# VectorE's order at the opening of a turn in a macaron block: two low parts, attention's sum, the statistics and layer 4's result change places

## The chip, the cores and the metric

The kernel runs on 1 core of one Trainium2 chip. The metric is the device time of one execution in microseconds (us). TensorE does the matmuls, VectorE and ScalarE read its banks in PSUM, GpSimd works in SBUF alone, SyncE issues transfers. In the views below they are PE (PEld for its weight loads), DVE, ACT, POOL and SP; "DVEq" is VectorE's queue, that is its sequencer's own instructions.

## The reference, cut to what matters

x has 8 sequences of 512 tokens with 128 features. The block is a feed-forward net, a recurrent layer in attention's place, and the same feed-forward net again, each behind a layer norm and each added to x:

```python
def ffn(x):                                  # D 128, hidden 512
    h = silu(tlin(x, w1, s1)) * tlin(x, w2, s2)
    h = gelu(tlin(h, h1, sh1)); h = gelu(tlin(h, h2, sh2))
    return tlin(h, w3, s3)
x = x + 0.5 * ffn(layernorm(x))
x = x + attn(layernorm(x))     # h = tanh(x_t B + h A^T) over the tokens; y = h C; y W_out^T + b
x = x + 0.5 * ffn(layernorm(x))
```

## The kernel before, in words

The 4096 tokens are cut into 8 chunks of 512 columns. Each chunk passes the feed-forward net twice: 16 passes, g = 0 to 15, called turns here. Features or hidden units lie on the partitions, the chunk's tokens on the columns. Every layer's matmul takes its input as two float32r parts, the high part (y_hi, rounded by ScalarE or VectorE) and the low part (y_lo = y - y_hi, a TENSOR_TENSOR of VectorE, L705 and L700, or of GpSimd, L1271 and L1265). Layers 2 and 3 have 4 rows m of 4 steps k with 2 matmuls each (L256), layer 1 has 4 rows with two products (th's and u's bank), layer 4 has one row of 4 steps.

The order of the work is written out by hand on each engine; there is no scheduler. Turn g runs layers 2 and 3 of chunk g and layer 1 of chunk g + 1, and at its opening layer 4 of chunk g - 1. On TensorE the opening is: layer 2's row 0 with steps k = 0 and 1, attention's two matmuls (`attention`, L395), step k = 2, layer 4 of the chunk before (L256 in bank F1), the transposes of the next chunk's tokens (`front_tokens`, L274, from attention's sum lnin to bank FR), step k = 3. Then come the scan's matmul for step 0 (L388), row 1, scan step 1, row 2 (which overwrites layer 4's bank F1 and therefore waits for layer 4's result, `l4_out`), scan step 2, the transposes of the normalised features (`to_features`, L284, from xnt_f), row 3. Steps k of row 0 wait for y1's high and low part k: 0 to 2 from GpSimd, 3 from VectorE (`low1`, L700). Layer 4's step 3 waits for y3's low part 3 (`low`, L705). The token transposes wait for attention's sum (L732).

There are four kinds of turns. First-round turns 0 to 5 (`first_turn`, `early_turn`) have no attention; they transpose x1c, layer 4's result of the first pass, for the middle norm (L264). Three middle turns (`middle_turn`, c = 0, 1, 2) have both; with c = 1 and 2 the opening has attention's sum and the front statistics. Then follow turns of the second pass (`turn`, k = 1 to 7): 1 written out, 2 to 5 in a loop whose waits are against registers, 6 and 7 written out. Turn 7 has no next chunk and no attention. "Turn 1" to "turn 7" below are these; the middle turns are named as such.

The scan of the recurrent layer runs beside: a matmul per step (L388), two tanh of ScalarE (L1042, L1043) and a low part of VectorE (L724), which the next step's matmul waits for; a turn has 8 of them.

The front statistics (`front_stats`, L646) are four bn_stats (L630), a memset and four bn_aggr (L635) on VectorE; GpSimd makes 1/sqrt(var + eps) of them (ve L1257, rs L1260), VectorE normalises (L663) into xnt_f. Layer 4's result (`layer4`, L707, with its instruction at L719) is 0.5 s3 times the bank plus the residual, written to x1c or outb, and SyncE sends it off. In the end, when the scan's blocks agree, no further round is run; the profiled execution runs one. In turn 6 VectorE also compares the scan's ends (L974, L978) ahead of attention's sum.

VectorE's side of the end of a turn (before) and of the opening of a turn:

```python
772  gated(g + 1, KT - 1)          # y1's last part of the next chunk
773  y1_high(g + 1, KT - 1)
774  low1(g + 1)                   # its low part, L700
775  low(g, 3, y3_hi_r, ...)       # y3's last low part, L705
854  attention(att[0], att[1])     # the sum, L732
856  layer4(1, g - 1, k - 1)       # the result, L719
858  front_stats(g + 1)            # L630, L635
859  step(0); step(1)              # the scan's low parts, L724
862  normalise("f", g + 1, ...)    # L663
```

Of the kernel before, what the change touches and what calls it, by code (L numbers as in the profile page):

```python
# [35 lines left out]
CHUNKS = 8  # L36
# [20 lines left out]
def build(nc, xT, xtok, w1T, w2T, h1T, h2T, w3T, scales, Ablk, Brep, CTrep, WoutT, ident_d, mask_d, outT):  # L57
    with ExitStack() as ctx:
# [568 lines left out]
        def _(dve):  # L627
# [70 lines left out]
            def low1(g):  # L698
                dve.wait_ge(y1_hi_r[KT - 1], g + 1)
                nc.vector.tensor_tensor(y1_lo[:, KT - 1, :], y1[:, KT - 1, :], y1_hi[:, KT - 1, :].bitcast(F32),  # L700
                                        ALU.subtract).then_inc(y1_lo_dve, 1)
# [20 lines left out]
            def scan_low(n, t):  # L722
                dve.wait_ge(step_t, n * CSTEPS + t + 1)
                nc.vector.tensor_tensor(h[0:64, span(t)], SC[0:64, span(CSTEPS + t)], h[0:64, span(t)].bitcast(F32),  # L724
                                        ALU.subtract).then_inc(step_h, 1)
# [44 lines left out]
            def end_turn(g):  # L770

                gated(g + 1, KT - 1)
                y1_high(g + 1, KT - 1)
                low1(g + 1)
                low(g, 3, y3_hi_r, y23, y3_hi, y3_lo, y3_lo_dve)

            def early_turn(g, mid, scan):
                def step(t):
                    if scan is not None and t is not None:
                        scan_low(scan, t)  # L780
                xn_low(g + 1)
                layer4(0, g - 1, g - 1)
                step(0)
                first_stats(g + 2)
                mean_negated(g + 2)
                middle_stats(mid)
                step(1)
                low(g, 1, y2_hi_r, y23, y2_hi, y2_lo, y2_lo_dve)
                step(2)
                normalise("m", mid, MI, mv_m, rs_m, xnt_m)  # L790
                step(3)
                low(g, 3, y2_hi_r, y23, y2_hi, y2_lo, y2_lo_dve)
                first_gates(g + 1, step, (4, None, 5, None))
                step(6)
                low(g, 1, y3_hi_r, y23, y3_hi, y3_lo, y3_lo_dve)
                step(7)
                low(g, 2, y3_hi_r, y23, y3_hi, y3_lo, y3_lo_dve)
                gate(g + 1, KT - 1)
                end_turn(g)

            def middle_turn(g, c):
                mid = g - 1

                def first_pass(t):
                    if c == 0:
                        scan_low(FIRST_PASS - 1, t)

                def step(t):
                    if t is not None:
                        scan_low(FIRST_PASS + c, t)  # L810
                if c == 0:
                    xn_low(g + 1)
                    layer4((g - 1) // CHUNKS, g - 1, (g - 1) % CHUNKS)
                    first_pass(0)
                    first_pass(1)
                    first_pass(2)
                    middle_stats(mid)
                    first_pass(3)
                    first_pass(4)
                    low(g, 1, y2_hi_r, y23, y2_hi, y2_lo, y2_lo_dve)  # L820
                    first_pass(5)
                    first_pass(6)
                    normalise("m", mid, MI, mv_m, rs_m, xnt_m)
                    first_pass(7)
                    restart(0)
                else:
                    attention(c - 1, c - 1)
                    layer4((g - 1) // CHUNKS, g - 1, (g - 1) % CHUNKS)
                    front_stats(g + 1)
                    normalise("f", g + 1, FR, mv_f, rs_f, xnt_f)  # L830
                    middle_stats(mid)
                    low(g, 1, y2_hi_r, y23, y2_hi, y2_lo, y2_lo_dve)
                    xn_low(g + 1)
                    normalise("m", mid, MI, mv_m, rs_m, xnt_m)
                low(g, 3, y2_hi_r, y23, y2_hi, y2_lo, y2_lo_dve)
                first_gates(g + 1, step, (None, 0, 1, 2))
                step(3)
                step(4)
                low(g, 1, y3_hi_r, y23, y3_hi, y3_lo, y3_lo_dve)
                step(5)  # L840
                step(6)
                low(g, 2, y3_hi_r, y23, y3_hi, y3_lo, y3_lo_dve)
                gate(g + 1, KT - 1)
                step(7)
                end_turn(g)

            def turn(k, g, att, scan, joined=True):
                last = isinstance(k, int) and k == CHUNKS - 1

                def step(t):  # L850
                    if scan is not None and t is not None:
                        scan_low(scan, t)
                if att is not None:
                    attention(att[0], att[1])
                if joined:
                    layer4(1, g - 1, k - 1)
                if not last:
                    front_stats(g + 1)
                step(0)
                step(1)  # L860
                if not last:
                    normalise("f", g + 1, FR, mv_f, rs_f, xnt_f)
                low(g, 1, y2_hi_r, y23, y2_hi, y2_lo, y2_lo_dve)
                step(2)
                if not last:
                    xn_low(g + 1)
                step(3)
                low(g, 3, y2_hi_r, y23, y2_hi, y2_lo, y2_lo_dve)
                if not last:
                    first_gates(g + 1, step, (4, None, 5, None))  # L870
                step(6)
                low(g, 1, y3_hi_r, y23, y3_hi, y3_lo, y3_lo_dve)
                step(7)
                low(g, 2, y3_hi_r, y23, y3_hi, y3_lo, y3_lo_dve)
                if not last:
                    gate(g + 1, KT - 1)
                    end_turn(g)
                else:
                    low(g, 3, y3_hi_r, y23, y3_hi, y3_lo, y3_lo_dve)
                    layer4(1, g, k)  # L880
# [57 lines left out]
            layer1(1, KT - 1)  # L938
            y1_high(1, KT - 1)
            low(0, 3, y3_hi_r, y23, y3_hi, y3_lo, y3_lo_dve)  # L940
            low1(1)
            early_turn(1, 0, None)
            early_turn(2, 1, 0)
            with dve.Fori(3, FIRST_PASS + 1) as k:
# [4 lines left out]
            def round_(r):  # L949
                gb = r * CHUNKS  # L950
                if isinstance(r, int):
                    middle_turn(CHUNKS, 2)
                else:
                    restart(r)
                    for t in range(CSTEPS):
                        scan_low(gb + FIRST_PASS, t)
                    attention(gb, 0)
                    front_stats(gb + CHUNKS)
                    normalise("f", gb + CHUNKS, FR, mv_f, rs_f, xnt_f)
                    for t in range(CSTEPS):  # L960
                        scan_low(gb + FIRST_PASS + 1, t)
                    xn_low(gb + CHUNKS)
                    attention(gb + 1, 1)
                    for m in range(KT):
                        layer1(gb + CHUNKS, m, late=True)
                    low1(gb + CHUNKS)
                    turn(0, gb + CHUNKS, None, gb + FIRST_PASS + 2, False)
                turn(1, gb + 1 + CHUNKS, (gb + 2, 2), gb + FIRST_PASS + 3)
                with dve.Fori(2, CHUNKS - 2) as k:
                    turn(k, gb + k + CHUNKS, (gb + k + 1, k + 1), gb + FIRST_PASS + k + 2)  # L970
                if isinstance(r, int):

                    dve.wait_ge(step_h, (FIRST_PASS + CHUNKS) * CSTEPS)
                    nc.vector.tensor_tensor(h_ne[:, :, :], by_seq(h_first[:, :].bitcast(F32))[:, :, 1:BLOCKS],  # L974
                                            by_seq(h[:, span(CSTEPS - 1)].bitcast(F32))[:, :, 0:BLOCKS - 1],
                                            ALU.not_equal).then_inc(h_ne_r, 1)
                    dve.wait_ge(h_ne_r, 1)
                    nc.vector.reduce_sum(h_nes[:, :], h_ne[:, :, :].rearrange("p s b -> p (s b)"),  # L978
                                         axis=mybir.AxisListType.X).then_inc(h_nes_r, 1)
                turn(CHUNKS - 2, gb + 2 * CHUNKS - 2, (gb + CHUNKS - 1, CHUNKS - 1), None)  # L980
                if isinstance(r, int):
                    dve.wait_ge(agree_mm, 1)
                    nc.vector.tensor_scalar(again[:, :], MI[0:1, 0:1], 0.0, None, ALU.is_gt).then_inc(again_r, 1)
                turn(CHUNKS - 1, gb + 2 * CHUNKS - 1, None, None)
# [456 lines left out]
```

## Time and profile before

| | |
|---|---|
| median of 3 runs | 409.53 us (409.25 to 409.66) |
| the profiled execution | 409.59 us, its span 407.7 us |
| TensorE (PE) busy | 385.1 us, 94% of the span |
| VectorE (DVE) busy | 275.1 us, 67% |
| ScalarE (ACT) busy | 270.4 us, 66% |
| GpSimd (POOL) busy | 165.6 us, 41% |
| mean granted TensorE clock | 0.981 |

Busy is time with an instruction at work; matmuls overlap, so a matmul's own time (some 0.40 us) is longer than the step to the next one. In the timeline a row has its start, its time, engine, line and operation, what it writes and reads, and a count where equal ones are merged; in brackets stands the idle time of the engine before it and who ended it. A semaphore's way and register operations of a queue are not busy time of an engine.

### The profile page before, as it was taken

The page shows a single profiled execution, that of the slowest core. Times are in us where ns is not written, and L with a number is a line of the kernel's source. Part 1 is how long each engine was busy: PE and PEld are TensorE (multiplying, and loading weights), DVE is VectorE, ACT ScalarE, POOL GpSimd, SP SyncE. Part 2 cuts the span into 40 slices and gives each one's busy share as a digit, 9 for nine tenths or more (in the row PEclk, how much of TensorE's full clock was granted, in tenths as well). Part 3 has the DMA queues.
Part 4 walks back from the last instruction along what each step waited for, and adds up shares of the span by engine and source line. Part 5 has one row for each costly group of instructions (what it writes and reads, how often), then busy time and mean ns, then how long its engine had stood idle before and what let it go on. Part 6 is the DMA issues. An engine that isn't in the chain of part 4 may idle for free.

```text
span 407.7 us, 6683 instructions
## 1 busy us (share of the span) xinstructions
PE 385.1 (94%) x1787; PEld 302.0 (74%) x1787; DVE 275.1 (67%) x726; ACT 270.4 (66%) x639; POOL 165.6 (41%) x156
## 2 busy tenths in 40 slices
PE   6868999999999999999999999999999999999980
PEld 4646787787878788777877778878787777877760
DVE  4784677777777767667768876757767776767421
ACT  3557767685868768576674767767575757757550
POOL 3433545261645536053551623535252343535210
PEclk9698999999999999999999999999999999999997
DMA  8900000000000000000101001010101001010001
GB/s 266 430 28 2 1 26 2 27 2 18 10 1 26 0 26 0 26 2 1 51 2 52 2 12 41 0 52 2 51 0 51 0 4 47 1 51 2 27 0 34
DMA packets 6078, 14.02 MB, mean 34 GB/s; under 512 B 1056, under 2 KB 1568, under 8 KB 5792
## 3 DMA queue, kind: packets, MB, share of 16 engines
q1 hardware_dynamic: 5040, 13.37, 8.5%
q10 hardware_dynamic: 1008, 0.29, 0.3%
q8 instruction: 13, 0.21, 0.2%
q14 instruction: 17, 0.14, 0.1%
HBM read 7.37 MB, written 2.10 MB: 23 GB/s over the span
## 4 chain that ended last, share of the span: by engine, by line
PE 81%; DVE 7%; ACT 4%; issue 3%; POOL 2%; DMA 1%; DVEq 0%; POOLq 0%; ACTq 0%
PE F L256 67%; PE FR L256 8%; PE FR L284 2%; DVE xnt_f L663 1%; POOL rs_f L1260 1%; PE SC L373 1%; DVE st_f L630 1%; DVE u L675 1%; ACT y_hi L1026 1%; DVE y L685 1%; PE MI L284 1%; DMA x_all<-in_xtok 1%; PE MI L264 1%; ACT th L1005 1%; ACT y L1023 1%
## 5 line engine op out<-in xcount | busy, mean ns | idle before, releaser
L256 PE MATMUL F<-y_hi,w_hi 128*128 128x512 f32 x512 | 211.9, 414 | 6.6 <-ACT y_hi L1026 2.5
L256 PE MATMUL F<-y_lo,w_hi 128*128 128x512 f32 x512 | 203.0, 396 | 0.0
L256 PEld LDWEIGHTS F<-y_hi,w_hi 128*128 128x128 f32 x512 | 96.6, 189 | 31.4 <-issue 6.5
L256 PEld LDWEIGHTS F<-y_lo,w_hi 128*128 128x128 f32 x512 | 97.0, 189 | 18.4
L1023 ACT ACTIVATE y<-F,sc 128x512 f32<-128x512 f32 x112 | 76.6, 684 | 48.5 <-PE F L256 48.0
L705 DVE TENSOR_TENSOR y_lo<-y,y_hi 128x512 fp32r<-128x512 f32 x80 | 65.0, 812 | 54.1 <-ACT y_hi L1026 54.1
L1265 POOL TENSOR_TENSOR y_lo<-y,y_hi 128x512 fp32r<-128x512 f32 x48 | 68.0, 1419 | 64.4 <-DVE y_hi L692 53.6
L1271 POOL TENSOR_TENSOR y_lo<-y,y_hi 128x512 fp32r<-128x512 f32 x48 | 62.1, 1302 | 35.8 <-ACT y_hi L1026 35.8
L1026 ACT ACTIVATE y_hi<-F,sc 128x512 fp32r<-128x512 f32 x112 | 76.5, 683 | 0.0
L1042 ACT ACTIVATE h<-SC 128x32 fp32r<-128x32 f32 x104 | 20.3, 195 | 55.6 <-PE SC L388 53.7
L256 PE MATMUL F<-xn_hi,w_hi 128*128 128x512 f32 x119 | 50.5, 425 | 1.9 <-POOL w_lo L1317 1.9
L256 PE MATMUL F<-xn_lo,w_hi 128*128 128x512 f32 x119 | 47.1, 396 | 0.0
L675 DVE SCALAR_TENSOR_TENSOR u<-th,F 128x512 f32<-128x512 f32 x61 | 41.6, 681 | 8.1 <-ACT th L1005 8.1
L1257 POOL TENSOR_TENSOR ve_f<-mv_f,epsc 128x4 f32<-128x4 f32 x16 | 3.2, 202 | 105.2 <-DVE mv_f L635 99.8
L1005 ACT ACTIVATE th<-F,s1h 128x512 f32<-128x512 f32 x61 | 40.9, 689 | 7.3 <-PE F L256 4.5
L685 DVE SCALAR_TENSOR_TENSOR y<-F,s12h,u 128x512 f32<-128x512 f32 x58 | 43.3, 747 | 1.7
L724 DVE TENSOR_TENSOR h<-SC,h 64x32 fp32r<-64x32 f32 x104 | 18.4, 177 | 21.4 <-ACT SC L1043 21.0
L256 PEld LDWEIGHTS F<-xn_hi,w_hi 128*128 128x128 f32 x119 | 22.6, 190 | 8.4 <-ACT w_hi L1168 2.1
L256 PE MATMUL FR<-y_hi,w_hi 128*128 128x512 f32 x64 | 26.0, 407 | 0.6 <-DVE y L685 0.6
L256 PEld LDWEIGHTS F<-xn_lo,w_hi 128*128 128x128 f32 x119 | 22.8, 191 | 3.5
L256 PE MATMUL FR<-y_lo,w_hi 128*128 128x512 f32 x64 | 25.3, 395 | 0.0
L388 PEld LDWEIGHTS SC<-h,a_mix 128*128 128x128 f32 x103 | 19.3, 188 | 6.1 <-DVE h L724 1.8
(123 smaller groups left out, 398.3 us busy)
## 6 DMA issues: line engine op xcount, KB each, us to landing
x_all<-in_xT SPq DMA_DIRECT2D x1, 2048.0 KB, 17.0
x_all<-x1c SPq DMA_DIRECT2D x8, 256.0 KB, 2.3
x_all<-lnin SPq DMA_DIRECT2D x8, 256.0 KB, 2.3
out<-outb SPq DMA_DIRECT2D x8, 256.0 KB, 2.0
x_all<-in_xtok SPq DMA_DIRECT2D x1, 1536.0 KB, 12.7
w_raw<-in_h1T SPq DMA_DIRECT2D x2, 512.0 KB, 7.5
w_raw<-in_h2T SPq DMA_DIRECT2D x2, 512.0 KB, 9.2
x_all<-in_xtok SPq DMA_DIRECT2D x2, 256.0 KB, 4.5
```

The source lines that it names most:

```text
L256: mm = nc.tensor.matmul(out, wtile(w, layer, k, m), y, start=first and i == 0, stop=last and i == len(pairs) - 1)
L388: nc.tensor.matmul(SC[:, span(t)], a_mix[:, :], states, start=False, stop=True, skip_group_check=True).then_inc(step_mm, 1)
L675: nc.vector.scalar_tensor_tensor(out=u[:, m % 2, :], in0=th[:, m % 2, :], scalar=1.0, in1=l1_banks(g, m, late)[0][:, :], op0=ALU.add, op1= ...
L685: nc.vector.scalar_tensor_tensor(out=y1[:, m, :], in0=l1_banks(g, m, late)[1][:, :], scalar=s12h[:, m:m + 1], in1=u[:, m % 2, :], op0=ALU. ...
L705: nc.vector.tensor_tensor(y_lo[:, k, :], y[:, k, :], y_hi[:, k, :].bitcast(F32), ALU.subtract).then_inc(out_sem, 1)
L724: nc.vector.tensor_tensor(h[0:64, span(t)], SC[0:64, span(CSTEPS + t)], h[0:64, span(t)].bitcast(F32), ALU.subtract).then_inc(step_h, 1)
L1005: nc.scalar.activation(th[:, m % 2, :], l1_banks(g, m, late)[0][:, :], ACT.Tanh, scale=s1h[:, m:m + 1]).then_inc(th_r, 1)
L1023: nc.scalar.activation(y23[:, m, :], bankt[:, :], ACT.Gelu, scale=s)
L1026: nc.scalar.activation(y_hi[:, m, :], bankt[:, :], ACT.Gelu, scale=s).then_inc(hi_r, 1)
L1042: nc.scalar.activation(h[:, span(t)], SC[:, span(t)], ACT.Tanh)
L1265: pool.tensor_tensor(y1_lo[:, m, :], y1[:, m, :], y1_hi[:, m, :].bitcast(F32), ALU.subtract).then_inc(y1_lo_pool, 1)
L1271: pool.tensor_tensor(y_lo[:, k, :], y[:, k, :], y_hi[:, k, :].bitcast(F32), ALU.subtract).then_inc(out_sem, 1)
```

## The change

VectorE's queue alone is rewritten. `low1`, y1's last low part, leaves the end of a turn and stands at the opening of the next one: first in first-round turns and in the first middle turn, behind attention's sum in the others (where there is no sum, first). So y3's last low part comes ahead of it. In turns with front statistics these now come ahead of layer 4's result. In middle turns 1 and 2, turn 0 of a further round and the turns 1 to 6 both apply. The start of the program and the further rounds lose their own `low1`, since the next opening has it.

```diff
@@ end_turn
                 gated(g + 1, KT - 1)
                 y1_high(g + 1, KT - 1)
-                low1(g + 1)
                 low(g, 3, y3_hi_r, y23, y3_hi, y3_lo, y3_lo_dve)
@@ early_turn
+                low1(g)
                 xn_low(g + 1)
                 layer4(0, g - 1, g - 1)
@@ middle_turn
                 if c == 0:
+                    low1(g)
                     xn_low(g + 1)
...
                 else:
                     attention(c - 1, c - 1)
+                    low1(g)
+                    front_stats(g + 1)
                     layer4((g - 1) // CHUNKS, g - 1, (g - 1) % CHUNKS)
-                    front_stats(g + 1)
                     normalise("f", g + 1, FR, mv_f, rs_f, xnt_f)
@@ turn
                 if att is not None:
                     attention(att[0], att[1])
+                low1(g)
+                if not last:
+                    front_stats(g + 1)
                 if joined:
                     layer4(1, g - 1, k - 1)
-                if not last:
-                    front_stats(g + 1)
                 step(0)
@@ the start
             low(0, 3, y3_hi_r, y23, y3_hi, y3_lo, y3_lo_dve)
-            low1(1)
             early_turn(1, 0, None)
@@ a further round
                     for m in range(KT):
                         layer1(gb + CHUNKS, m, late=True)
-                    low1(gb + CHUNKS)
                     turn(0, gb + CHUNKS, None, gb + FIRST_PASS + 2, False)
```

## Rows read from the trace of the kernel before

**Rows 1.** The page's chain that ended last, shares of the span by engine

```profile
PE 81%; DVE 7%; ACT 4%; issue 3%; POOL 2%; DMA 1%; DVEq 0%; POOLq 0%; ACTq 0%
```

**Rows 2.** Timeline, middle turn 1 at its opening (start us, us, engine, line, operation)

```profile
192.23 0.69 DVE L705 TENSOR_TENSOR y_lo<-y,y_hi 128x512 fp32r<-128x512 f32 x1
192.66 0.39 PE L256 MATMUL F<-y_lo,w_hi 128*128 128x512 f32 x1
193.06 0.48 PE L256 MATMUL F<-y_hi,w_hi 128*128 128x512 f32 x1
193.38 0.39 PE L256 MATMUL F<-y_lo,w_hi 128*128 128x512 f32 x1
...
193.63 0.66 PE L274 MATMUL FR<-ident,lnin 128*128 128x128 f32 x4
...
196.47 0.60 PE L264 MATMUL MI<-ident,x1c 128*128 128x128 f32 x4
```

**Rows 3.** Timeline, PE, turn 3 of the loop

```profile
288.50 0.40 PE L256 MATMUL F<-y_lo,w_hi 128*128 128x512 f32 x1
...
288.89 0.65 PE L274 MATMUL FR<-ident,lnin 128*128 128x128 f32 x4
...
291.84 0.18 PE L388 MATMUL SC<-h,a_mix 128*128 128x32 f32 x1
...
294.21 0.66 PE L284 MATMUL FR<-ident,xnt_f 128*128 128x128 f32 x4 [0.21 <-DVE xnt_f L663]
```

**Rows 4.** Timeline, turn 1: scan step 1 to the transposes of xnt_f

```profile
245.98 0.18 PE L388 MATMUL SC<-h,a_mix 128*128 128x32 f32 x1
...
246.52 0.18 DVE L724 TENSOR_TENSOR h<-SC,h 64x32 fp32r<-64x32 f32 x1 [1.28 <-ACT SC L1043]
246.63 1.35 DVE L663 TENSOR_SCALAR xnt_f<-FR,mv_f,rs_f 128x128 f32<-128x128 f32 x4
...
248.04 0.66 PE L284 MATMUL FR<-ident,xnt_f 128*128 128x128 f32 x4
```

**Rows 5.** Timeline, VectorE and one of ScalarE, turn 3 of the loop

```profile
286.03 0.68 ACT L1026 ACTIVATE y_hi<-F,sc 128x512 fp32r<-128x512 f32 x1
...
287.32 0.69 DVE L705 TENSOR_TENSOR y_lo<-y,y_hi 128x512 fp32r<-128x512 f32 x1
...
287.92 0.74 DVE L732 SCALAR_TENSOR_TENSOR lnin<-MI,sc,x_all 128x512 f32<-128x512 f32 x1
...
289.24 0.75 DVE L719 SCALAR_TENSOR_TENSOR outb<-F,s3h,x_all 128x512 f32<-128x512 f32 x1 [0.58 <-PE F L256]
...
289.91 0.88 DVE L630 BATCH_NORM_STATS2 st_f<-FR 128x6 f32<-128x128 f32 x4
...
291.13 0.15 DVE L724 TENSOR_TENSOR h<-SC,h 64x32 fp32r<-64x32 f32 x1
...
292.78 1.37 DVE L663 TENSOR_SCALAR xnt_f<-FR,mv_f,rs_f 128x128 f32<-128x128 f32 x4 [0.23 <-POOL rs_f L1260]
```

**Rows 6.** Chain of waits in order of time, turn 3 (start us, us, what)

```profile
286.56 2.35 PE F L256 x10
...
289.13 0.06 DVEq L719
```

**Rows 7.** Timeline, turn 6 at its opening

```profile
357.67 0.75 DVE L732 SCALAR_TENSOR_TENSOR lnin<-MI,sc,x_all 128x512 f32<-128x512 f32 x1
...
357.87 0.40 PE L256 MATMUL F<-y_lo,w_hi 128*128 128x512 f32 x1
...
358.47 0.66 PE L274 MATMUL FR<-ident,lnin 128*128 128x128 f32 x4 [0.20 <-DVE lnin L732]
```

**Rows 8.** GpSimd's ve of the middle statistics (ns min/median/max), then timeline, first round

```profile
L1257 POOL TENSOR_TENSOR ve_m<-mv_m,epsc x8: 201/601/648, 57.4 to 224.5; 128x4 f32<-128x4 f32 x8
...
64.33 0.75 DVE L685 SCALAR_TENSOR_TENSOR y<-F,s12h,u 128x512 f32<-128x512 f32 x1
...
64.49 1.30 POOL L1265 TENSOR_TENSOR y_lo<-y,y_hi 128x512 fp32r<-128x512 f32 x1 [2.94 <-DVE y_hi L692]
```

## The prediction, made before the changed kernel was built or timed

> **What bounds the kernel now.** I read the chain of waits first. It runs almost wholly through TensorE's layer matmuls [rows 1]: what makes TensorE wait is paid in full, and what happens behind its back costs nothing. The change only reorders VectorE, so the question is where TensorE waits for VectorE at the opening of a turn. The timeline shows three places, all in turns that carry attention's sum.
>
> First, middle turns 1 and 2 and turn 1 of the round, whose gaps agree to 0.01 us; middle turn 1 stands for them. Layer 4's sixth matmul of eight starts at 192.66. At the pitch of 0.235 (ten in 2.35 us [rows 6]) and the 0.25 from the eighth to the transposes of the next tokens (193.38 to 193.63), these would start at 193.38. But the seventh comes at 193.06, behind y3's last low part (192.23 + 0.69 = 192.92), and the transposes at 193.63 [rows 2]. That is 0.25 us lost in each of 3 turns.
>
> Second, the four turns of the loop (turns 2 to 5). There y3's last low part is in time. But from the scan's matmul at 291.84 to the transposes of the normalised features at 294.21 it takes 2.37 us [rows 3], where turn 1 needs 2.06 for the same work (245.98 to 248.04) [rows 4]. The other three loop turns repeat this to 0.02 us. So 0.31 us is a wait for xnt_f. Going back from it: the statistics start at 289.91, 1.02 behind the token transposes' start at 288.89, although those end at 289.54. In between stands layer 4's result, from 289.24 [rows 3, 5]. It started 0.34 behind the matmuls' end, because three register operations of the queue stand between the wait and it [rows 6].
>
> Third, turn 6: attention's sum lies behind two low parts and the comparison of the scan's ends and is done at 358.42. The transposes start at 358.47, 0.60 behind the matmul before them, where 0.25 is undisturbed [rows 2, 7]. 0.35 us lost.
>
> **The change part by part.** No instruction is added or removed; only VectorE's queue is reordered, and in-order waits move with it.
>
> (a) y3's last low part goes ahead of y1's. y1's took 0.60 start to start [rows 5], so y3's can start 0.60 sooner in the middle turns. In the loop it must await y3_hi, done at 286.71 [rows 5]; it then starts at some 286.8 instead of 287.32. Gain: the whole 0.25 in each of 3 turns. I take 0.24, 0.24 and 0.22, as turn 1 then comes near the scan bound of (c): 0.70. Bounds 0.55 and 0.75. In the loop's turns it frees nothing directly.
>
> (b) Attention's sum comes sooner by 0.5 to 0.6 and y1's low part comes behind it, about 1.3 later. Now a low part is queued behind the wait for attention's matmuls. Those are issued behind layer 2's second k step, ahead of layer 4; the sum starts 0.60 behind the low part in front of it, the engine's own pace, so they were done [rows 5]. Layer 2's fourth step is the one waiting for y1's low part. In the loop: y3's low 286.8, sum 287.4, y1's low 288.1, done 288.8; TensorE gets to the fourth step only behind the transposes that start at 288.89. In the middle turns y3's low starts at 191.63, the sum 0.60 and y1's low 0.67 later; it ends at about 193.6, and the transposes would start at 193.38 and take 0.4 until the next matmul can follow: 0.2 to spare. In turn 6 the sum moves up with y3's low part by 0.52, as in the loop, to 357.15 and is done at 357.9, the transposes start at 358.12, and y1's low ends at 357.15 + 0.67 + 0.69 = 358.5, about when the fourth step could follow the transposes; I charge 0.06. Net gain in turn 6: 0.35 - 0.06, and about as much back where its statistics also come sooner: 0.35; bounds 0.25 and 0.45. In the loop the transposes come 0.39 behind the last matmul (288.50) against 0.25 in middle turns. With the sum done at 288.66, that may be a wait for it or the four register waits in front of the transposes. Bounds 0 and 0.14; I take 0.05, near the register end, because those waits remain: 4 x 0.05 = 0.20.
>
> (c) Statistics ahead of layer 4's result. Write T for the start of the token transposes. They end at T+0.65, a direct wait takes 0.03 to 0.1 more: statistics at T+0.70 instead of T+1.02. By this path alone xnt_f's transposes would come 0.32 sooner, at T+5.00. But layer 4's result now starts behind nine small instructions, 1.22 after the statistics' start (289.91 to 291.13) [rows 5], at T+1.92. Its four register operations may lie bare there; from 0 to 0.40 (the three in front of it cost 0.30 more than the 0.03 of a bare wait). I take 0.10, because the scan's low part, with one such operation, followed the aggregations without a gap: T+2.02. The scan's low part follows 0.67 later (289.24 to 289.91), takes 0.16, and TensorE's next scan matmul can come at T+2.90 to T+2.95. It came at T+2.95 (291.84): no loss. Layer 4's result itself is written at T+2.77, and layer 2's third row, which overwrites its bank, starts at T+2.97: no loss either. Then the scan sets the pace: its second low part comes 0.54 behind its matmul (246.52 against 245.98), the normalisation 0.11 behind that [rows 4], and its transposes 1.43 later (292.78 to 294.21). That is 2.08, and I add 0.09, about one register operation, for the loop: 2.17 against 2.37. Gain 0.20 in each of 4 turns, 0.80. Bounds per turn: with all register operations bare the scan slips by 0.25 to 0.3 and the turn loses 0.06; with none it gains the full 0.31. So -0.24 and +1.24.
>
> In middle turns x1c is now written at about T+2.65 and its transposes were at 196.47, T+2.84 [rows 2]: 0.15 or so to spare. Its save and the output's DMA, on SP's queue, go out 1.7 us later (1.22 + the change of start); the next issue behind them is that of the next turn's sum, 20 us on, so I cost it at nothing.
>
> (d) The first-round turns and the last turn: only the swap of low parts. The fourth k step has layer 4's eight matmuls at 0.23 in front of it as cover (1.9 us against the 0.6 by which y1's low is later). Value zero; the nearest row for a gain is 0.25 once, in the last turn.
>
> One rule is weighed here. GpSimd's ve, which takes 0.20 at its quickest, takes 0.60 in the median right behind the middle statistics, where the next VectorE instruction is a low part of two SBUF inputs [rows 8]. Now layer 4's result stands behind the front statistics, beside ve_f and rs_f. It reads PSUM and one SBUF tile, like y at 64.33, beside which a GpSimd low part kept its 1.30 [rows 8]. So I cost it at nothing. The Trainium skill, GPSIMD Engine Reference, section 1 (Specifications), says that GpSimd's SBUF interfaces are shared with VectorE, with contention for instructions with two SBUF inputs or in a 2-port mode. By it the result costs nothing as long as no 2-port mode is at work; if it were, the sum would be that of the third rival.
>
> **Sum**: 0.70 + 0.35 + 0.20 + 0.80 = 2.05 us. The profiled execution took 409.59 (span 407.7 and 1.9 around it); 409.59 - 2.05 = 407.54. The median of the runs, 409.53, is 0.06 lower: 407.5. The ends: 0.55 + 0.25 + 0 - 0.24 = 0.56, giving 409.0; and 0.75 + 0.45 + 0.56 + 1.24 + 0.25 = 3.25, giving 406.3.
>
> **The rivals.**
> First: the scan takes the place of the statistics' wait. In the loop, the normalisation stands behind the second scan low part, and this behind a matmul that needs the first, which now stands behind layer 4's result. If the register operations lie bare, (c) is worth 0 and (b)'s 0.20 too: 1.05 saved, 408.5. For it: the margin is 0 to 0.05. Against: turn 1's rows, where no gap shows. 18%.
>
> Second, slower: layer 4's result too late. Place: TensorE's second scan matmul and the bank that layer 2's third row overwrites (in middle turns the x1c transposes). It decides when the result starts 0.6 later than computed. Then the scan slips by 0.57 and each loop turn ends 0.37 behind before (1.48); two middle turns and turn 1 lose 0.3 net each (0.84 to 0.9); turn 6 keeps 0.35: 2.0 slower, 411.5. Against: the worst row for register operations is 0.34. 5%.
>
> Third: GpSimd is held by the result as by a low part, 0.36 to 0.4 per turn. Statistics' path then gives T+5.38 in the loop, nothing gained there, and the middle turns lose most of theirs: about 0.7 saved, 408.8. 6%.
>
> Fourth: the waits read as VectorE's are really something else and nothing moves: 409.5. 6%.
>
> **How the numbers follow.** My forecast 65%, the rivals 18, 5, 6 and 6. A measurement can tell 0.2% here, 0.8 us, so the borders are 408.7 and 410.35. Faster: 65, 13 of the first rival's 18 and little of the third's: 0.79. Same: 0.16. Slower: 0.05. The range reaches from 406.5, short of the lower end, to 409.1, over the first and third rivals.
>
> **What would show it.** In the middle turns the matmul behind 192.66 should follow at 0.23 and the token transposes at once. In the loop the statistics should start about 0.7 behind the token transposes, rs_f be released 0.3 sooner, layer 4's result start right behind the aggregation, and TensorE's idle time before the xnt_f transposes shrink from 0.23 to under 0.1, with xnt_f now released by the scan's low part rather than by rs_f. Idle time of TensorE's weight loads before the second scan matmul (for h) would show the first rival; before layer 2's third row or the x1c transposes, the second; a ve_f of 0.5 or more, the third. I am wrong if in turns 2 to 5 the transposes of xnt_f still come 2.37 or more behind the scan's matmul.

## The result, and the profile after

The changed kernel took 405.44 us in the median of 4 runs (404.26 to 405.76), the kernel before 409.39 on the same chip (408.67 to 409.66): a ratio of 0.9901, 95% interval 0.9877 to 0.9925. The forecast was 407.5, in a range from 406.5 to 409.1. The direction was right; the gain was 3.95 us instead of 2, and the time lies below the range. Of this, 3.4 us are the change's own in the profiles and the rest is the start of the program, as the repeated runs show below. Three of the later executions took 473, 747 and 946 us, far from all others; the ratios below leave them out, the medians keep them.

The profiled execution took 404.26 us with a span of 402.3. The page's chain that ended last, of the changed kernel (before: [rows 1]):

```profile
PE 88%; DVE 4%; ACT 3%; issue 1%; POOL 1%; DMA 1%; ACTq 0%; DVEq 0%
```

VectorE's share fell from 7% to 4% and TensorE's rose from 81% to 88%: the pieces that ran over VectorE at the openings are gone. The chain of waits in order of time, turn 3 of the changed kernel (before it ran over layer 4's result, the statistics, rs_f and xnt_f [rows 6]; columns: start us, us, what):

```profile
283.33 2.33 PE F L256 x10
285.66 0.44 PE FR L274 x4
286.10 0.54 PE F L256 x2
286.64 0.02 PE SC L388
286.66 1.95 PE F L256 x8
288.61 0.04 PE SC L388
288.65 1.96 PE F L256 x8
290.61 0.02 PE SC L388
290.63 0.54 PE FR L284 x4
```

From the attention matmuls to row 3 it never leaves TensorE. Now the same places as in the prediction. The opening of middle turn 1, timeline of the changed kernel (start us, us, engine, line, operation; before: [rows 2]):

```profile
189.51 0.43 DVE L692 CAST y_hi<-y 128x512 fp32r<-128x512 f32 x1
189.85 0.68 DVE L705 TENSOR_TENSOR y_lo<-y,y_hi 128x512 fp32r<-128x512 f32 x1
190.46 0.74 DVE L732 SCALAR_TENSOR_TENSOR lnin<-MI,sc,x_all 128x512 f32<-128x512 f32 x1
191.02 0.39 PE L256 MATMUL F<-y_lo,w_hi 128*128 128x512 f32 x1
191.25 0.39 PE L256 MATMUL F<-y_hi,w_hi 128*128 128x512 f32 x1
191.48 0.39 PE L256 MATMUL F<-y_lo,w_hi 128*128 128x512 f32 x1
191.48 0.59 PEld L274 LDWEIGHTS FR<-ident,lnin 128*128 128x128 f32 x4
191.71 0.60 PE L274 MATMUL FR<-ident,lnin 128*128 128x128 f32 x4
192.06 0.48 PE L256 MATMUL F<-y_hi,w_hi 128*128 128x512 f32 x1
```

The seventh matmul of layer 4 follows the sixth at 0.23 (191.02, 191.25), and the transposes at 191.71. Two things go further than forecast. y3's low part starts 0.34 behind the cast in front of it. And the transposes take 0.35 until the next matmul can start, not the 0.41 of before: lnin was there long ahead, so their weights were loaded while matmuls still ran (191.48). In the kernel before, the same load waited for lnin, which was done at 193.57 (timeline, middle turn 1):

```profile
191.16 0.43 DVE L692 CAST y_hi<-y 128x512 fp32r<-128x512 f32 x1
191.62 0.69 DVE L700 TENSOR_TENSOR y_lo<-y,y_hi 128x512 fp32r<-128x512 f32 x1
...
193.63 0.42 PEld L274 LDWEIGHTS FR<-ident,lnin 128*128 128x128 f32 x4 [0.30 <-DVE lnin L732]
```

Turn 3 of the loop, timeline of the changed kernel, VectorE, TensorE and GpSimd (before: [rows 3, 5]):

```profile
283.51 0.69 DVE L705 TENSOR_TENSOR y_lo<-y,y_hi 128x512 fp32r<-128x512 f32 x1
284.44 0.75 DVE L732 SCALAR_TENSOR_TENSOR lnin<-MI,sc,x_all 128x512 f32<-128x512 f32 x1 [0.24 <-issue]
285.11 0.68 DVE L700 TENSOR_TENSOR y_lo<-y,y_hi 128x512 fp32r<-128x512 f32 x1
285.27 0.39 PE L256 MATMUL F<-y_lo,w_hi 128*128 128x512 f32 x1
285.50 0.60 PE L274 MATMUL FR<-ident,lnin 128*128 128x128 f32 x4
285.94 0.47 PE L256 MATMUL F<-y_hi,w_hi 128*128 128x512 f32 x1
286.14 0.89 DVE L630 BATCH_NORM_STATS2 st_f<-FR 128x6 f32<-128x128 f32 x4 [0.35 <-PE FR L274]
287.48 0.75 DVE L719 SCALAR_TENSOR_TENSOR outb<-F,s3h,x_all 128x512 f32<-128x512 f32 x1
287.53 0.20 POOL L1258 TENSOR_TENSOR ve_f<-mv_f,epsc 128x4 f32<-128x4 f32 x1 [6.50 <-DVE mv_f L635]
287.89 1.01 POOL L1261 TENSOR_TENSOR rs_f<-ve_f,mhalf 128x4 f32<-128x4 f32 x1 [0.16 <-POOL ve_f L1258]
288.14 0.17 DVE L724 TENSOR_TENSOR h<-SC,h 64x32 fp32r<-64x32 f32 x1
288.37 0.19 PEld L388 LDWEIGHTS SC<-h,a_mix 128*128 128x128 f32 x1 [0.19 <-DVE h L724]
288.45 0.20 PE L388 MATMUL SC<-h,a_mix 128*128 128x32 f32 x1
289.00 0.18 DVE L724 TENSOR_TENSOR h<-SC,h 64x32 fp32r<-64x32 f32 x1 [0.68 <-ACT SC L1044]
289.10 1.35 DVE L663 TENSOR_SCALAR xnt_f<-FR,mv_f,rs_f 128x128 f32<-128x128 f32 x4
290.51 0.66 PE L284 MATMUL FR<-ident,xnt_f 128*128 128x128 f32 x4
```

The transposes come 0.23 behind the last matmul, not 0.39. The statistics start 0.64 behind them, not 1.02; the result stands 1.34 behind the statistics' start; the scan's second matmul comes at T+2.95, exactly where it was, though its weight load now waits 0.19 for h; and from there to the xnt_f transposes it is 2.06 instead of 2.37. ve_f, beside the result, took its 0.20. In the other three loop turns the scan's second matmul comes at T+2.90 to T+2.92 and the rest takes 2.09 to 2.11, so that in all four the xnt_f transposes come at T+5.01.

One thing went the other way. Attention's sum starts 0.93 behind y3's low part (283.51, 284.44), not 0.60, with 0.24 of idle time in which the queue waited for nothing that the profile shows; its own register waits stand there. So y1's low part is done only at 285.79, and TensorE's fourth step starts at 285.94, 0.44 behind T, where 0.35 is undisturbed. It is 0.38 to 0.41 in the other loop turns and 0.50 in turn 6.

All turns side by side. A turn runs here from its attention matmuls (L395) to the next turn's; T is the start of the token transposes; the numbers are differences of starts in the timelines, in us.

| turn | L395 to T, before / after | T to xnt_f's transposes | length | gain | forecast |
|---|---|---|---|---|---|
| middle 1 | 2.84 / 2.56 | 5.16 / 5.08 | 24.71 / 24.29 | 0.42 | 0.24 |
| middle 2 | 2.83 / 2.57 | 5.16 / 5.07 | 24.69 / 24.29 | 0.40 | 0.24 |
| 1 | 2.84 / 2.56 | 5.01 / 4.94 | 22.85 / 22.51 | 0.34 | 0.22 |
| 2 | 2.72 / 2.56 | 5.31 / 5.01 | 23.13 / 22.70 | 0.43 | 0.25 |
| 3 | 2.72 / 2.56 | 5.32 / 5.01 | 23.11 / 22.67 | 0.44 | 0.25 |
| 4 | 2.72 / 2.57 | 5.32 / 5.00 | 23.14 / 22.70 | 0.44 | 0.25 |
| 5 | 2.70 / 2.56 | 5.32 / 5.01 | 23.12 / 22.71 | 0.41 | 0.25 |
| 6 and 7, to the last matmul | 2.93 / 2.56 | 4.83 / 4.79 | 42.80 / 42.27 | 0.53 | 0.35 |

Together 3.41 us. The first-round turns, from the xnt_f transposes of turn 0 (49.33 before, 47.67 after) to middle turn 1, are equal to 0.02. So the 1.64 us by which the profiled executions differ beyond that stand ahead of any work that the change touches.

### The profile page after: what moved, and what is told of

Its sections match the earlier page's. It is cut to its first block, busy times and chain, and to the rows that moved or that the text cites. A ratio compares the mean times of both kernels' runs of the same rounds, so it can differ in the third digit from the quotient of the medians.

```text
span 402.3 us, 6690 instructions
## 1 busy us (share of the span) xinstructions
PE 379.5 (94%) x1787; PEld 300.5 (75%) x1787; DVE 275.7 (69%) x726; ACT 270.3 (67%) x639; POOL 165.4 (41%) x156
## 4 chain that ended last, share of the span: by engine, by line
PE 88%; DVE 4%; ACT 3%; issue 1%; POOL 1%; DMA 1%; ACTq 0%; DVEq 0%
PE F L256 73%; PE FR L256 8%; PE FR L284 2%; PE SC L373 1%; PE MI L284 1%; PE MI L264 1%; PE FR L274 1%; DMA x_all<-in_xtok 1%; DVE u L675 1%; ACT th L1006 1%; ACT y L1024 1%; DVE y L685 1%; ACT xnt_f L1063 1%; ACT y_hi L1027 1%; POOL w_lo L1318 1%
```

## The experiments

Two measures stand beside each other below: the device time, and **the trace's measure**, from the start of the first round's xnt_f transposes (L284, near 48) to the start of the last matmul. The latter was 349.01 before and 345.62 after; it leaves the start of the program out.

**Both kernels again.** No edit. For the kernel before, the expectation was:

> The kernel before, unchanged, to part the change's gain from what the start of the program does by itself. In the two profiles at hand, 1.64 us of the difference stand ahead of the first turn that the change touches (the transposes of turn 1 of the first round start at 49.33 before and at 47.67 after), and 3.41 us lie behind it (from there to the last matmul: 349.01 before, 345.62 after). Theory A: the start varies by itself and the change is worth 3.4 us. Then this run has 349.0 from those transposes to the last matmul to within 0.1, while their start may differ from 49.33 by up to 1.5 us; ratio 1.000. Theory B: the start too is a gain of the change (its code lies otherwise in memory). Then the transposes start at 49.3 again, within 0.2.

For the changed kernel, in the second group of runs:

> The changed kernel, unchanged. Theory A (the start varies by itself, with the place of the stretch of low granted clock in the first 35 us; the change is worth 3.4 us, all behind the first round): from the transposes of turn 1 of the first round to the last matmul 345.6 to within 0.1, those transposes anywhere from 47.6 to 49.4, a ratio of 0.9915 to before. Theory B (the start belongs to the change): the transposes at 47.7 again with the clock of 0.79 between 8 and 16 us, a ratio of 0.990 or less.

Measured: before 409.36 us against 408.96 for its partners, ratio 1.0005 (0.9988 to 1.0023), the trace's measure 349.00, those transposes at 48.85. The changed kernel 405.85 against 408.38, ratio 0.9940 (0.9923 to 0.9957), the measure 345.63, the transposes at 48.42. The trace's measure repeats to 0.01 in both kernels, as theory A has it. (Two of the profiles below lose 0.4 us just behind its starting point; it is said there.) The start moved by 0.48 and 0.75 between two executions of one kernel, and in the experiments below, kernels with the changed order started between 47.9 and 48.9, which overlaps with the 48.85 of before. In the device times of all groups the medians of before were 409.39, 408.96 and 408.38, and the 8 runs of the changed kernel have a median of 405.64: some 3.3 us. So the start is no gain of the change on average; that a tenth or two of it is can't be excluded by so few profiles. Part of what moves it shows in the granted clock. TensorE's clock for 8 to 16 us and for 24 to 34 us of the span, first the kernel before, then the changed one (busy times of the engines, then the clock, DMA share and GB/s):

```profile
8.00:16.00 8.00, 5.50 (x17) 4.41 (x18) 4.88 (x20) 2.94 (x7) 4.52 (x4) 0.64 1.05 419
...
24.00:34.00 10.00, 6.69 (x24) 4.80 (x23) 7.60 (x28) 4.81 (x9) 3.58 (x5) 0.84 0.01 2
```

```profile
8.00:16.00 8.00, 5.77 (x21) 4.61 (x22) 5.76 (x20) 3.79 (x7) 4.52 (x4) 0.79 1.04 416
...
24.00:34.00 10.00, 7.23 (x32) 5.60 (x33) 7.83 (x27) 5.26 (x10) 3.66 (x6) 1.00 0.01 2
```

From 11 us on layer 1 of chunk 0 runs, and in the two executions TensorE was granted a mean of 0.64 and 0.79 of its full clock, that is its lower level for some 5.8 and 3.4 of the 8 us; the changed kernel's profiled execution had more of the full level in both stretches. Its repetition had 0.79 and 0.84, and those transposes at 48.42. The clock is not all of it: the kernel before repeated with 0.64 and 0.83, hardly different from its 0.64 and 0.84, and still started 0.48 sooner, 0.40 of it ahead of the first transposes of chunk 0 (8.18 instead of 8.58). What moves those is not known. The two ratios, 0.9901 and 0.9940, lie on both sides of the 0.9917 that 3.4 us make, so of the 3.95 us of the first comparison about half a microsecond is the start.

**The low parts swapped alone.** Against the kernel before:

```diff
-                low1(g + 1)
                 low(g, 3, y3_hi_r, y23, y3_hi, y3_lo, y3_lo_dve)
+                low1(g + 1)
```

> The kernel before with y3's last low part ahead of y1's, both still at the end of the turn, attention's sum behind both. Theory A (it is the sum that sets the token transposes, y3's low part only the matmul ahead of them): middle turns 1, 2 and turn 1 gain only what the missing wait of y1's low part for its own high part gives, 0.12 each, since the sum still ends two low parts later; the loop's turns lose 0.05 each; together 0.2 us faster, 409.2 if before is 409.4. Theory B (y3's low part alone was what those turns waited for, as the prediction had it): 0.25 each, 0.75 us faster or more.

Measured: 408.28 us, ratio 0.9989 (0.9973 to 1.0006), not told from no change; the trace's measure 348.42, so 0.59 faster. The middle turns and turn 1 gained 0.19, 0.19 and 0.14, of which 0.13 ahead of T; the loop's turns nothing (23.12, T at 2.75 instead of 2.72). Timeline, middle turn 1 of this kernel:

```profile
190.40 0.68 DVE L705 TENSOR_TENSOR y_lo<-y,y_hi 128x512 fp32r<-128x512 f32 x1
191.00 0.69 DVE L700 TENSOR_TENSOR y_lo<-y,y_hi 128x512 fp32r<-128x512 f32 x1
191.60 0.75 DVE L732 SCALAR_TENSOR_TENSOR lnin<-MI,sc,x_all 128x512 f32<-128x512 f32 x1
192.03 0.40 PE L256 MATMUL F<-y_lo,w_hi 128*128 128x512 f32 x1
192.41 0.66 PE L274 MATMUL FR<-ident,lnin 128*128 128x128 f32 x4
```

Layer 4's matmuls run at their pitch (192.03 behind 191.80), but the transposes now come 0.38 behind the last of them, right behind lnin (191.60 + 0.75 = 192.35). The wait moved from y3's low part to attention's sum, and only 0.13 was won, the time that y1's low part had waited for VectorE's own cast. Theory A's mechanism holds; its total was 0.4 too small, since the middle turns won another 0.06 each behind T, turns 6 and 7 as much, and the loop's turns lost nothing. So in the middle turns and turn 1 it was attention's sum, done 0.06 ahead of the transposes, that set T, and not y3's low part, as the prediction read it.

**y1's low part behind the sum, the result still ahead of the statistics.** Against the changed kernel:

```diff
                 low1(g)
-                if not last:
-                    front_stats(g + 1)
                 if joined:
                     layer4(1, g - 1, k - 1)
+                if not last:
+                    front_stats(g + 1)
```

and the same in `middle_turn`.

> The changed kernel, but layer 4's result again ahead of the statistics: the first half of the change alone. Theory A (the parts add up): the token transposes come 0.28 sooner in three turns with 0.06 more because their weights are loaded ahead, 0.16 sooner in the four loop turns, 0.35 in turn 6, and the wait of 0.31 for xnt_f in the loop stays: 2.0 us faster than before. Rival (the halves need each other: what the transposes gain is waited for again at xnt_f, as the statistics stay behind the result): 1.3 us faster, with the idle time before the xnt_f transposes grown to 0.4.

Measured: 406.98 us, ratio 0.9954 (0.9937 to 0.9970); the trace's measure 347.63, 1.38 faster. The rival is right in its time, though TensorE's idle time before the loop's xnt_f transposes is 0.25 to 0.32 (before 0.21 to 0.23) and not the 0.4 expected. T comes 0.28 sooner in middle turns and turn 1, 0.16 sooner in the loop, 0.36 sooner in turn 6, as forecast. But the loop's turns are only 0.07 to 0.11 shorter, and turn 6 gives back 0.23 (T to xnt_f's transposes 5.06 instead of 4.83). Timeline, turn 3 of this kernel:

```profile
286.42 0.62 PE L274 MATMUL FR<-ident,lnin 128*128 128x128 f32 x4
286.93 0.75 DVE L719 SCALAR_TENSOR_TENSOR outb<-F,s3h,x_all 128x512 f32<-128x512 f32 x1 [0.21 <-issue]
287.60 0.88 DVE L630 BATCH_NORM_STATS2 st_f<-FR 128x6 f32<-128x128 f32 x4
290.38 1.37 DVE L663 TENSOR_SCALAR xnt_f<-FR,mv_f,rs_f 128x128 f32<-128x128 f32 x4 [0.26 <-POOL rs_f L1261]
291.81 0.66 PE L284 MATMUL FR<-ident,xnt_f 128*128 128x128 f32 x4 [0.25 <-DVE xnt_f L663]
```

The statistics start at T+1.18, later behind the transposes than the 1.02 of before, because they hang on layer 4's result and this on the matmuls ahead of T. So part of what T wins is waited for again, here over rs_f. In the middle turns, which are 0.18 longer than in the changed kernel, the wait comes at the middle norm's transposes instead (timeline, middle turn 1 of this kernel; in the changed kernel that load waits for nothing):

```profile
201.24 0.42 PEld L284 LDWEIGHTS MI<-ident,xnt_m 128*128 128x128 f32 x4 [0.27 <-DVE xnt_m L663]
```

**The statistics first, alone.** Against the kernel before, the mirror image of that edit (`front_stats` ahead of `layer4`, `low1` still at the end of the turn).

> The kernel before with the statistics ahead of layer 4's result alone: the second half. Theory A: 0.31 in each of the four loop turns, nothing in middle turns and turn 1, 0.07 in turn 6: 1.3 us faster; the time from the scan's second matmul to the xnt_f transposes falls from 2.37 to 2.06. Rival (the register waits in front of the result and of the normalisation lie bare, the prediction's terms): 0.8 us faster, with 2.17.

Measured: 407.75 us, ratio 0.9977 (0.9961 to 0.9992); the trace's measure 348.43, but some 0.4 was lost against the kernel before in the first 6.4 us behind its starting point, ahead of the changed turns and right behind a stretch, 34 to 50 us, in which TensorE's granted clock was 0.89 instead of 1.00. Behind that 0.98 were won: 0.21, 0.14, 0.25 and 0.23 in the loop, 0.10 and 0.06 in the middle turns, 0.01 in turn 1. T to the xnt_f transposes fell from 5.32 to 5.07 in the loop. That lies between the theory's 1.3 and the rival's 0.8, and so does the time from the scan's second matmul to the transposes, 2.12 to 2.14. The scan's matmul holds the difference (timeline, turn 3 of this kernel):

```profile
291.37 0.25 PE L388 MATMUL SC<-h,a_mix 128*128 128x32 f32 x1
```

Its row is 0.25 long instead of 0.18, so part of it is the wait for h, and the low part that follows comes 0.60 behind it instead of 0.54. Behind that low part the normalisation follows at 0.10, so the register waits in front of it are hidden, as theory A has it.

The two halves alone make 1.38 + 0.98 = 2.36 us, together 3.4. One us is won only with both: 0.5 in the loop and 0.3 in turns 6 and 7, where T's gain needs statistics that don't wait for the result, and 0.2 in the middle turns, where the same shows at the middle norm's transposes.

**The loop written out.** Turns 2 to 5 of the changed kernel, on TensorE, VectorE, ScalarE and GpSimd:

```diff
-                with dve.Fori(2, CHUNKS - 2) as k:
-                    turn(k, gb + k + CHUNKS, (gb + k + 1, k + 1), gb + FIRST_PASS + k + 2)
+                if isinstance(r, int):
+                    for k in range(2, CHUNKS - 2):
+                        turn(k, gb + k + CHUNKS, (gb + k + 1, k + 1), gb + FIRST_PASS + k + 2)
+                else:
+                    with dve.Fori(2, CHUNKS - 2) as k:
+                        turn(k, gb + k + CHUNKS, (gb + k + 1, k + 1), gb + FIRST_PASS + k + 2)
```

> The changed kernel with turns 2 to 5 of the first round written out on TensorE, VectorE, ScalarE and GpSimd instead of looped (the loops of further rounds stay). Theory A (register waits in front of TensorE's transposes and steps are what is left between a loop turn, 22.70 us, and turn 1, 22.51): 0.19 in each of four turns, 0.75 us faster than the changed kernel, 344.9 from the first transposes to the last matmul. Rival (those register operations are hidden by the matmuls in flight, the difference being something else, or code that runs only once must be fetched and waits for that): no change, or slower, with idle time of the engines by 'issue' in the written-out turns.

Measured: 404.57 us, ratio to before 0.9908 (0.9893 to 0.9923), against 405.85 for the changed kernel in the same group; the trace's measure 344.79, 0.84 less than the changed kernel's 345.63. It is the fastest version here. Each written-out turn takes 22.50. Busy times over turn 2 of it (length, TensorE, its weight loads, VectorE, ScalarE, GpSimd, clock, DMA share, GB/s):

```profile
260.97:283.47 22.50, 22.50 (x108) 18.42 (x106) 16.17 (x41) 15.56 (x41) 9.28 (x8) 1.00 0.07 24
```

Theory A holds in the time: 0.2 per turn was the price of the loop. But T stands 0.23 behind layer 4's last matmul in both kernels, so none of it is paid in front of TensorE's token transposes. 0.08 lie between T and the xnt_f transposes (4.93 instead of 5.01), and there they come from VectorE: attention's sum follows y3's low part at 0.61, y1's low part is done 0.04 ahead of T and the fourth step starts at T+0.36; layer 4's result starts at T+1.86 instead of T+1.97. The other 0.12 lie behind the xnt_f transposes and were not traced to an engine; nor does this run part register waits from the loop's own instructions. Fetching the longer code shows as no wait in these turns, where TensorE is busy throughout.

**The result delayed.** To measure the margin of the slower rival, two copies of a y1 tile go between the front statistics and the result in every turn that has both:

```diff
+            def padding():
+                for i in range(2):
+                    nc.vector.tensor_copy(pad[:, i, :], y1[:, 0, :])
...
                     front_stats(g + 1)
+                    padding()
```

> The changed kernel with two copies of one y1 tile (0.34 us each, start to start) on VectorE between the front statistics and layer 4's result, to measure how near the rival of a late result is. Theory A (no slack in the loop's turns: the scan's second matmul is released just in time by the low part behind the result): the loop's turns grow by 0.65, turn 1 by 0.55, the two middle turns by 0.5 (x1c's transposes had 0.15 to spare), turn 6 by 0.35: 350.1 from the first transposes to the last matmul instead of 345.6. Rival (more slack than that, at least 0.3 per turn): the loop's turns grow by 0.35 or less.

Measured in one execution: 410.38 us, the trace's measure 350.33 (350.1 was expected). 0.39 of it were lost ahead of the changed turns, as in the run with the statistics first, and with the same granted clock of 0.89 from 34 to 50 us; without them it is 349.9. The scan's second matmul came at T+3.40 instead of T+2.9 in turn 1 and in the loop, the xnt_f transposes at T+5.54 instead of T+5.01, and x1c's transposes waited too. TensorE's waits in this kernel (who for whom, us in total, times, longest):

```profile
PE SC L389 <- DVE h L729: 1.8, 5, 0.4
...
PE MI L265 <- DVE x1c L720: 0.7, 2, 0.4
```

Two copies, 0.65 us long, cost 0.50 to 0.55 per loop turn and 0.59 in middle turns and turn 1 (24.88 and 23.10 instead of 24.29 and 22.51), and 0.44 in turns 6 and 7. The result started at T+2.51 instead of T+1.97 in the loop, 0.54 later, and the xnt_f transposes came 0.53 later: no margin there. In turn 1 0.65 became 0.59, a margin of 0.06. From the first middle turn on, this delay makes the kernel 0.9 us slower than the one before (349.9 against 349.0): two thirds of a microsecond at this one place outweigh the whole change. Theory A holds, though its 0.65 per loop turn left out that the copies cover 0.11 of register operations in front of the result.

**The same delay, the scan ahead of it.** As before, and in `turn`:

```diff
                     padding()
+                step(0)
                 if joined:
                     layer4(1, g - 1, k - 1)
-                step(0)
                 step(1)
```

> As r7, with the scan's first low part moved ahead of layer 4's result in the turns of the second pass (the copies still ahead of both). Theory A (it is the scan that a late result holds up, the bank that layer 2's third row overwrites comes next): the scan's second matmul is on time again (0.96 and 2.95 behind the token transposes, give or take 0.05) and row 3 of layer 2 waits for the result instead, 0.45 per loop turn, 0.2 less than in r7. Rival (the bank, not the scan, held r7 up): the loop's turns as long as in r7.

Measured in one execution: 409.41 us, the trace's measure 349.37. The scan's second matmul is back at T+2.88 to T+2.90, and TensorE waits for outb, as its waits in this kernel show:

```profile
PE F L257 <- DVE outb L720: 1.9, 6, 0.3
```

A loop turn took 23.12, 0.42 more than in the changed kernel and 0.11 less than in the run before. Theory A holds, with half its difference: the scan is the nearer limit. Here the result starts 0.10 later than in the run before, behind the scan's low part (T+2.61), and the xnt_f transposes still come 0.15 sooner (T+5.39); by these two the bank that layer 2's third row overwrites is a limit some 0.25 behind the scan's, an estimate.

## Why the prediction was off

**Right.** The three places stand, and two of the causes: the statistics behind the result in the loop, attention's sum in turn 6. In the middle turns and turn 1 the prediction laid all 0.25 to y3's low part; that held up layer 4's seventh matmul, but T hung on attention's sum, as the swap alone showed (0.13 instead of 0.25). The change moved both, so the gain came all the same. The statistics now start 0.64 behind T (0.70 forecast), the scan's low part took over as xnt_f's releaser, y1's low part behind the sum made TensorE's fourth step wait 0.15 in turn 6 (354.08, 0.50 behind T, where 0.35 is undisturbed; 0.06 was charged) and 0.03 to 0.09 in the loop's turns, where nothing was charged. GpSimd's ve_f kept its 0.20 beside the result, so the third rival is out, and the rule on instructions with two SBUF inputs did not bite here. The first rival's mechanism was at work, and "the margin is 0 to 0.05" was right: the result in front of the scan's low part sets the loop's pace, but only 0.08 per turn hung on it. The slower rival's mechanism is real and its place too (the scan first, then the bank), as the delayed runs show. It begins to cost at once in the loop and 0.06 further on in turn 1, and its price with the result 0.54 to 0.65 later was 0.9 us slower than before, where the prediction had 2.0 at 0.6.

**Wrong: the size, term by term** (forecast 2.05, measured 3.4).

- (c), the register allowance: 0.80 forecast, some 1.2 measured. The step that failed is "I add 0.09, about one register operation, for the loop: 2.17 against 2.37". It took 2.06 to 2.11, 2.05 with the loop written out, and the transposes came at T+5.01, not at T+5.12: the wait for rs_f's semaphore no longer came last, and with nothing to wait for, the register operations ran while the scan's low part did (the normalisation starts 0.10 to 0.11 behind that, looped or written out). The 0.10 taken for the result was about right (1.34 instead of 1.22 behind the statistics' start), but it was not "no loss": written out, the result starts 0.11 and the transposes come 0.08 sooner.
- (b), the tokens in the loop: 0.20 forecast, 0.62 measured (0.16, 0.16, 0.15, 0.14). "I take 0.05, near the register end, because those waits remain" was wrong: the matmuls in flight cover them once lnin is early, and T follows the last matmul at 0.23 in the loop as when written out. Even its upper bound of 0.14 per turn was a little short.
- (a), the middle turns and turn 1: 0.70 forecast, 1.16 measured, beyond the bound of 0.75. Ahead of T it was 0.28 each rather than 0.25. Behind T another 0.07 to 0.08 came from the transposes, whose weights could be loaded early. And 0.06 per middle turn came behind the xnt_f transposes; the changed kernel's weight loads wait 0.2 us in total for xnt_m, where the kernel before had 0.8 us. With the result ahead of the statistics that load waited 0.27 again, and the middle turns were 0.18 longer.
- Turn 6: 0.35 forecast, 0.41 measured. Against these, the loop's turns gave back 0.12 together behind the xnt_f transposes, which no term had and no run explains.
- (d), the last turn: 0 forecast with 0.25 as bound, 0.12 measured.
- The start: half a microsecond of the 3.95 is no part of the change, and the prediction, made from one profiled execution and three runs, gave it no width.

The common fault: register operations were charged at the two places where they had shown bare in a chain, in front of the token transposes and of the normalisation. There the wait ahead of them no longer came last, and they vanished with it. They did show bare at a place that was not charged, in front of attention's sum (0.24 in the loop), which cost up to 0.09 at the fourth step; so it is not a rule that they vanish, it has to be asked place by place.

## What to carry to other kernels

When an in-order queue holds a result that is late by nature (here layer 4's) ahead of work that feeds the critical chain, swap them, and swap both ends of the chain at once: each half alone won 1.4 and 1.0 us, both 3.4. Price queue operations at nothing where the wait in front of them is no longer the last, and take them whole where it is. After such a swap, measure the new margin by a delay of known size; here there was none left in the loop and 0.06 us in turn 1.

## What the runs showed of the hardware that was not expected

- An instruction of VectorE that waits for the semaphore of the instruction right in front of it starts 0.46 behind the start of a 0.43 us cast (191.16 to 191.62 before); one that needs nothing of it starts 0.34 behind (189.51 to 189.85 after).
- Four 128x128 transposes hold TensorE for 0.35 us until the next matmul's start when their source was ready early (lnin done 0.51 ahead of them, middle turn 1 after), for 0.41 when it came late (0.06 ahead, middle turn 1 before).
- GpSimd's ve_f, a 128x4 instruction, took 0.29 us beside the two copies between 128x512 tiles in SBUF (the kernel with the result delayed) and 0.20 beside layer 4's result.
- From the first round's xnt_f transposes to the last matmul two executions of one kernel agree to 0.01 us in 349 (but two other kernels lost 0.4 us in the first turn behind that point, both with a granted clock of 0.89 from 34 to 50 us), while the first 50 us differ by 0.5 and 0.75 us between two executions of one kernel (49.33 and 48.85 before, 47.67 and 48.42 for the changed one), with TensorE's granted clock at 0.64 in the first two and 0.79 in the others from 8 to 16 us.
